# A macaron block's first layer: a new order of its slots, split sums for two of the FFN's products, and a norm moved to ScalarE

## The chip, the cores and the metric

The kernel runs on one core of a Trainium2 chip. The metric is the device time of one execution in microseconds. The core has TensorE (PE), VectorE (DVE), ScalarE (ACT), GpSimd (POOL) and SyncE (SP), which here only issues DMAs. Each engine runs its own list of instructions in order, and they meet through semaphores. All inputs and outputs are f32. About 0.2% (2 us) is what a measurement of this kernel can tell from no change.

## The reference, cut to what matters

```python
x = x + 0.5 * ffn0(layernorm(x))          # shared FFN with 8 LoRA experts, top 2
x = x + attn0(layernorm(x))               # gated linear attention, MLP behind it
x = x + 0.5 * ffn0(layernorm(x))
x = x + 0.5 * moe(layernorm(x))           # 8 experts, top 1
x = x + attn1(layernorm(x))
x = x + 0.5 * moe(layernorm(x))

def ffn0(x):                              # D=128, F=512, E=8, R=16, K=2
    t = rmsnorm(x) * norm_w
    probs = softmax(t @ gate_w.T)         # the best two, renormalised
    h1 = t @ w1.T + 2 * (t @ a1[e].T) @ b1[e].T
    h3 = t @ w3.T + 2 * (t @ a3[e].T) @ b3[e].T
    act = silu(h1) * h3
    out_e = act @ w2.T + 2 * (act @ a2[e].T) @ b2[e].T
    return sum over the two experts of weight_e * out_e
```

attn0 has the gates i, f = sigmoid(h @ Wi + bi), sigmoid(h @ Wf + bf) and o = sigmoid(h @ Wo + bo); its scores are a recurrence along the sequence. There are 4096 tokens of 128 values: eight sequences of 512. The output is x.

## The kernel before, in words

Tokens are worked on in chunks of 512, one sequence each, and x stays in SBUF. The first layer is the first three lines of the reference. Its two ffn0 passes over 8 chunks make 16 FFN items; the attention of a chunk lies between its two FFN items. All of it is one software pipeline: `SLOTS` holds slots m = -2 to 18, and `Slot` (line 56) says which item of which stage a slot works on: statistics (`stat`, item m+2), routing to the experts (`pre`, m+1), the products (`main`, m), the end of the item before (`tail`, m-1), six stages of attention (m-1 to m-6), and three of the second layer's routing (m-9 to m-11). So slots 6 to 9 hold everything of the attention, slots from 9 on also the routing, and slots 16 to 18 only ends.

The order within a slot is written out by hand, once for each engine: PE from line 623, ACT from line 999, DVE from line 1365, POOL from line 1711. A step there is a call such as `h(1, 3)`; each begins with its semaphore waits, so an engine that waits in one step holds up all steps behind it. SP loads x and all weights at the start, then zeroes the DRAM rows into which the routing scatters (line 309), then feeds the expert tiles.

For an FFN item, `h(1, k)` and `h(3, k)` (line 383) make h1 and h3 for step k of eight: four 128-row blocks j of F times two choices e. The choices are not computed per expert: u = a1 @ t for all 8 x 16 adapter rows is multiplied with a mask of the chosen expert (`ua` for the first choice) and by the difference of the two masks (`ud`), so that the second choice only adds its difference on top of the first in PSUM. These products are made in f32r with operands split into a high and a low part: `mm3` (line 361) is high*high + high*low + low*high. ACT makes silu, DVE `act(k)` (line 1190) multiplies with h3 and then with the choice's weight `wT`.

The two weighted activations of a block j, `act_[0][j]` and `act_[1][j]`, are then used in three ways, all in plain f32: POOL adds them to `gsum` (`total`, line 1639) and PE multiplies it with w2 (`down(j)`, line 425, bank BOUT); PE multiplies the first with a2 (`value(0, ...)`, first values, at the end of the slot) and the second with a2 (`value(1, ...)`, second values, in the next slot). DVE masks the values of either choice into `r1` and `r2`, POOL adds them, PE multiplies with b2 (`lora_out`), the result is transposed back and DVE adds half of it to x.

```python
def mm3(dst, w, m, start, stop, **more):
    mm(dst, w[0], m[0], start=start, stop=False, **more)
    mm(dst, w[0], m[1], start=False, stop=False, **more)
    return mm(dst, w[1], m[0], start=False, stop=stop, **more)
```

For the item one ahead, DVE normalises the rows (`f_norm`, line 1205, first in its slot), PE transposes them (`pre_T`), ACT saves them as f32 and as the high part, POOL makes the low part (`low`). PE makes `logits`, DVE picks the two experts (`top2`), ACT makes their weights from a tanh (`slot_weights`), PE transposes the choices into masks (`mask`), ACT saves them, POOL makes their difference (`mask_diff`), PE makes u (`up`), DVE masks it (`masked`), ACT and POOL split it (`up_high`, `up_low`).

For attention, `a_gate(0..3)` (line 593) makes the three gates and the values on PE, all through bank BSIDE each after ACT has saved the one before (`a_gates`, line 964, sigmoid); `a_scans` on DVE runs the recurrences; `a_den`, `a_back`, `a_mix` divide and add; `a_mid_T`, `a_mid`, `a_out`, `a_out_back` are the MLP. Routing has `r_norm`, `r_T`, `r_aff`, `r_top1`, `r_rank`, `r_rows`, `r_scatter`. PSUM has eight banks: two for h1, two for h3, BV (4) for values and the routing's transposes, BSIDE (5) for attention and routing, BOUT (6), BPRE (7) for the item ahead.

After the slots come small products of the second layer's weights (`products`), 23 expert tiles, the second attention and 23 tiles again.

## Time and profile before

| what | us |
|---|---|
| median of 3 runs | 1050.17 (1050.05 to 1051.02) |
| the profiled execution's own time | 1054.69 |
| its span, first to last instruction | 1053.0 |
| PE busy in it | 980.6 (93%) |
| DVE busy | 711.2 (68%) |
| ACT busy | 507.9 (48%) |
| POOL busy | 500.1 (47%) |
| mean granted TensorE clock | 0.992 of full speed |

Busy is the time in which an engine had an instruction under way. Matmuls are pipelined: a matmul's span is longer than the distance to the next one's start, so what PE takes for one is read from starts. In the trace an f32 matmul stands as two instructions, an f32r one as one. A number in brackets after an instruction is the engine's idle time before it with what ended it.

### The profile page before, as it was taken

How to read it: one execution, taken by the hardware profiler on the slowest of the kernel's cores; microseconds unless marked ns; L12 is line 12 of the kernel's file. 1: busy time of each engine (PE TensorE's matmuls, PEld its weight loads, DVE VectorE, ACT ScalarE, POOL GpSimd, SP SyncE). 2: the span in 40 equal slices, each digit the busy share in tenths (PEclk: the TensorE clock that was granted, in tenths of full speed). 3: DMA queues.
4: the chain of work that ended last, by engine and by line, in shares of the span. 5: the costliest groups of instructions: out<-in, count | busy, mean ns of one | idle time of the engine just before them, and what ended most of it. 6: DMA issues, size and time to landing. Idle time of an engine off the chain costs nothing. (4 is left out here: it accounts for less than half of the span.)

```text
span 1053.0 us, 15574 instructions
## 1 busy us (share of the span) xinstructions
PE 980.6 (93%) x4429; PEld 669.9 (64%) x4429; DVE 711.2 (68%) x2140; ACT 507.9 (48%) x1039; POOL 500.1 (47%) x485
## 2 busy tenths in 40 slices
PE   3999999999999999999999999899988999889993
PEld 2766667656565665656566656477864667648873
DVE  5787779788786877879797776445543667634542
ACT  3433454655646556564453332144534777515451
POOL 3456555554535545354654655524451155423443
PEclk9999999999999999999999999999999999989997
DMA  6069000000000000000000002146534000015651
GB/s 181 1 284 415 3 1 1 1 1 1 1 0 2 0 1 1 1 0 1 12 3 9 11 11 71 39 137 197 166 94 140 1 22 22 22 42 178 194 174 34
DMA packets 42900, 65.12 MB, mean 62 GB/s; under 512 B 7153, under 2 KB 25121, under 8 KB 40640
## 3 DMA queue, kind: packets, MB, share of 16 engines
q1 hardware_dynamic: 37824, 55.59, 16.1%
q0 software_dynamic: 4992, 8.54, 2.4%
q8 instruction: 36, 0.59, 0.2%
q14 instruction: 48, 0.39, 0.1%
HBM read 37.20 MB, written 28.74 MB: 63 GB/s over the span
## 5 line engine op out<-in xcount | busy, mean ns | idle before, releaser
L362 PE MATMUL bank<-split 128*128 128x512 f32 x416 | 206.9, 497 | 7.8 <-DVE ud L1267 4.1
L364 PE MATMUL bank<-split 128*128 128x512 f32 x416 | 165.2, 397 | 0.0
L363 PE MATMUL bank<-split 128*128 128x512 f32 x416 | 164.8, 396 | 0.0
L863 ACT ACTIVATE sil<-bank 128x512 f32<-128x512 f32 x128 | 76.2, 595 | 116.0 <-PE bank L364 115.2
L1644 POOL TENSOR_TENSOR gsum<-act 128x512 f32<-128x512 f32 x64 | 84.9, 1327 | 81.5 <-DVE act L1203 81.4
L421 PE MATMUL bank<-act,a 128*128 128x512 f32 x256 | 117.6, 592 | 0.0
L362 PEld LDWEIGHTS bank<-split 128*128 128x128 f32 x416 | 79.5, 191 | 48.8 <-issue 17.4
L1199 DVE TENSOR_TENSOR act<-bank,sil 128x512 f32<-128x512 f32 x128 | 87.8, 686 | 17.2 <-PE bank L364 14.2
L363 PEld LDWEIGHTS bank<-split 128*128 128x128 f32 x416 | 79.9, 192 | 28.3 <-issue 18.6
L688 PE MATMUL bank<-xlT,e 128*128 128x256 f32 x368 | 91.2, 392 | 5.1 <-ACT xlT L1068 2.7
L1203 DVE TENSOR_TENSOR act<-act,wT 128x512 f32<-128x512 f32 x128 | 91.7, 716 | 4.4
L364 PEld LDWEIGHTS bank<-split 128*128 128x128 f32 x416 | 79.2, 190 | 18.1
L704 PE MATMUL bank<-hT_e,e 128*128 128x256 f32 x368 | 87.3, 380 | 1.1 <-DVE oT_e L1534 1.1
L1068 ACT ACTIVATE xlT<-bank,lnb,lng 128x256 f32<-128x256 f32 x46 | 25.9, 564 | 119.0 <-PE bank L696 119.0
L1747 POOL DMA_INDIRECT rows_in<-yw,slot_i x64 | 62.9, 983 | 34.7 <-issue 18.8
L688 PEld LDWEIGHTS bank<-xlT,e 128*128 128x128 f32 x368 | 67.9, 194 | 16.5 <-issue 4.5
L1754 POOL DMA_INDIRECT out<-ob,ids x46 | 45.2, 983 | 66.9 <-DVE ob L1542 57.1
L1754 POOL DMA_INDIRECT rows_out<-ob,ids x46 | 45.2, 983 | 63.4 <-DVE ob L1542 55.6
L421 PEld LDWEIGHTS bank<-act,a 128*128 128x128 f32 x256 | 47.5, 190 | 42.0 <-issue 33.7
L704 PEld LDWEIGHTS bank<-hT_e,e 128*128 128x128 f32 x368 | 66.7, 191 | 8.7 <-issue 1.5
L431 PE MATMUL bank<-gsum,w 128*128 128x512 f32 x128 | 65.2, 600 | 0.5 <-POOL gsum L1644 0.5
L1529 DVE TENSOR_SCALAR hT_e<-bank,eb1T 128x256 f32<-128x256 f32 x92 | 40.3, 479 | 27.6 <-PE bank L688 27.2
(283 smaller groups left out, 1957.6 us busy)
## 6 DMA issues: line engine op xcount, KB each, us to landing
e<-e_dram SPq DMA_DIRECT2D x92, 256.0 KB, 3.1
rows_in<-yw SPq DMA_DIRECT2D x17, 1056.0 KB, 17.8
xin<-rows_in SPq DMA_DIRECT2D x46, 132.0 KB, 3.0
x<-rows_out SPq DMA_DIRECT2D x8, 256.0 KB, 4.7
rows_in<-yw,slot_i POOLq DMA_INDIRECT x64, 2.3
rows_out<-ob,ids POOLq DMA_INDIRECT x46, 2.3
out<-ob,ids POOLq DMA_INDIRECT x46, 2.4
act<-b_dram SPq DMA_DIRECT2D x2, 256.0 KB, 3.1
```

Of the source, the lines that this page charges most:

```text
L362: mm(dst, w[0], m[0], start=start, stop=False, **more)
L363: mm(dst, w[0], m[1], start=False, stop=False, **more)
L364: return mm(dst, w[1], m[0], start=False, stop=stop, **more)
L421: last = mm(bank[BV][:, :], a2[:, j, :], act_[e][j][:, :], start=j == 0, stop=j == J - 1)
L431: mm(bank[BOUT][:, :], w2[:, j, :], gsum[j % 2][:, :], start=j == 0, stop=False).then_inc(w2_used.sem, 1)
L688: last = mm(bank[2 * p + j // 2][:, (j % 2) * Q:(j % 2 + 1) * Q], w[:, rows(j)], xlT[p][:, :], start=True, stop=True)
L704: last = mm(bank[4][:, 0:Q], w[:, j, :], hT_e[p][:, j, :], start=j == 0, stop=j == J - 1)
L863: af(sil[(k - 1) % 2][:, :], bank[BH1[STEPS[k - 1][0] % 2]][:, :], ACT.Silu).then_inc(silu_done.sem, 1)
L1199: v.tensor_tensor(a[:, :], bank[BH3[j % 2]][:, :], sil[(k - 1) % 2][:, :], ALU.mult).then_inc(act_done.sem, 1)
L1203: v.tensor_tensor(a[:, :], a[:, :], wT[g % 2][e][:, :], ALU.mult).then_inc(weighted.sem, 1)
L1644: pool.tensor_tensor(out=gsum[j % 2][:, :], in0=act_[0][j][:, :], in1=act_[1][j][:, :], op=ALU.add).then_inc(summed.sem, 1)
L1754: pool.indirect_dma_start((rows_out, o)[n3 // NT], bass.IndirectOffsetOnAxis(ids[n3 % 4][:, q:q + 1], 0), ob[n3 % 4][:, q, :], None, bound ...
```

## The change

It does the following; the rest of the kernel, from the expert tiles on, is as before.

- The sum of the two weighted activations is written over the second (`act1[j]`), and ACT and POOL split it into a high and a low part (`sums_high`, `sums_low`). `down` and the second values use it with split w2 and a2 in three f32r passes. The second values are made of the sum: with masks m0 and m1, r = m1 * (a2 @ sum) - (m1 - m0) * (a2 @ first). First values are masked with the difference `mdT`.
- `down` for blocks 2 and 3 moves to the next slot, ahead of the second values.
- w2 and a2 are split in slot 0 (`sum_weights`, `sum_weights_low`).
- `f_norm` moves from DVE to ACT, at the end of the slot before, as x * scale + bias, with a product on POOL for the bias.
- The gates are sigmoid(z) = 0.5 * tanh(z/2) + 0.5: a tanh from PSUM (`gates_saved`), then a copy in place with scale and bias (`gates_done`). They are spread over the slot's second half.
- The MLP of the attention goes through BV, the routing's transposes through BSIDE.
- The order of each engine's slot is new. On POOL the row scatter moves to the next slot.
- `constants_for_routing` runs before the first slot instead of behind slot 1; the rows' zeroing follows slot -1 instead of slot 0. The weights of the second attention and the expert biases are loaded after the last slot's h (`late_loads`), into room that the split weights held.

```diff
+        LOW_DVE, LOW_POOL, LOW_LATE = (0, 1, 3, 5), (2, 4), (6, 7)
...
+                def value_sum():
+                    if l is None:
+                        return
+                    pe.wait_ge(*r_done(l, 1))
+                    pe.wait_ge(*sum_low(l))
+                    if l == 0:
+                        pe.wait_ge(weight_rest.sem, len(LOW_POOL) + 2)
+                    for j in range(J):
+                        last = mm3(bank[BV][:, :], tuple(w[:, rows(j)] for w in a2s), gs[j], j == 0, j == J - 1)
+                    last.then_inc(v_ready.sem, 1)
...
-                    pe.wait_ge(*summed(g, j + 1))
-                    mm(bank[BOUT][:, :], w2[:, j, :], gsum[j % 2][:, :], start=j == 0, stop=False).then_inc(w2_used.sem, 1)
+                    pe.wait_ge(*sum_low(n, j + 1))
+                    mm3(bank[BOUT][:, :], tuple(w[:, rows(j)] for w in w2s), gs[j], j == 0, False)
```

PE's order (its `fill` steps, which do something only from slot 16 on, left out):

```diff
-                h(1, 1); h(3, 1)
+                h(1, 1)
+                pre_T()
+                h(3, 1)
                 a_T()
                 h(1, 2)
+                logits()
+                if q == 0:
+                    up(0); up(1)
+                down(l, 2)
+                h(3, 2)
                 a_den()
-                h(3, 2)
-                pre_T()
+                down(l, 3)
+                value_sum()
                 a_back()
-                value(1, range(J))
                 h(1, 3)
                 r_aff()
                 h(3, 3)
-                logits()
                 a_out()
                 h(1, 4); h(3, 4)
                 lora_out()
                 a_out_back()
-                h(1, 5); h(3, 5)
+                h(1, 5)
+                mask(0)
+                h(3, 5)
                 back()
                 a_mid_T()
                 r_T()
+                mask(1)
                 h(1, 6)
                 a_mid(0)
+                mask(2)
                 h(3, 6)
-                mask(0)
-                down(0)
+                down(g, 0)
+                a_gate(0)
+                h(1, 7)
+                if q != 0:
+                    up(0)
                 a_mid(1)
-                h(1, 7)
-                mask(1)
                 h(3, 7)
+                down(g, 1)
+                a_gate(1)
                 a_mid(2)
-                down(1)
-                mask(2)
                 r_rank()
                 h(1, 8)
                 if q != 0:
-                    up(0)
+                    up(1)
+                a_gate(2)
                 h(3, 8)
-                value(0, (0, 1))
-                a_gate(0)
-                if q != 0:
-                    up(1)
-                value(0, (2, 3))
-                a_gate(1)
-                down(2)
-                a_gate(2)
-                down(3)
+                value((0, 1))
                 a_gate(3)
+                value((2, 3))
```

New or changed on ACT (guards for slots without the item left out):

```diff
+                def sums_high(n, j):
+                    act.wait_ge(*summed(n, j + 1))
+                    act.wait_ge(*v_ready(n - 1))
+                    af(gs[j][0], act1[j][:, :], ACT.Copy).then_inc(sum_high.sem, 1)
...
+                def f_norm():
+                    act.wait_ge(*rstd_f(n))
+                    act.wait_ge(*ynT_f(n - 1))
+                    for t in range(T):
+                        last = af(yn_f[:, t, :], xc(n)[:, t, :], ACT.Identity, bias=nb_f[n % 2][:, t:t + 1], scale=sc_f[n % 2][:, 1, t:t + 1])
...
+                    af(dst[:, :], bank[BSIDE][:, :], ACT.Tanh, bias=half[:, i:i + 1], scale=0.5).then_inc(gates_saved.sem, 1)
+                    act.wait_ge(*gates_saved(n, i + 1))
+                    af(dst[:, :], dst[:, :], ACT.Copy, scale=0.5, bias=0.5).then_inc(gates_done.sem, 1)
```

The new orders, whole, several steps to a line. ACT:

```
silu(1); pre_T(); sums_high(l, 3); a_T(); silu(2); sum_weights(); a_mid_norm(); silu(3); a_norm(0)
r_norm(s.r_pre) if s.m <= MAINS; slot_weights(); a_out(); silu(4); out_T(); silu(5)
sums_high(g, 0); mask(0); a_mid_T(); r_alpha(s.r_sort); r_T(s.r_pre, BSIDE); mask(1); silu(6)
sums_high(g, 1); a_mid(0); mask(2); mask(3); a_gate(0); silu(7); a_mid(1); a_gate(1); a_mid(2)
silu(8); up_high(0); a_gate(2); up_high(1); f_norm(); a_norm(1); sums_high(g, 2)
a_square(0); a_square(1); a_square(2); r_norm(s.r_stat) if s.m >= MAINS
```

DVE:

```
r_factors(s.r_pre); act(1); split_low(LOW_DVE[:2]); top2(0); act(2); a_den(); top2(1)
split_low(LOW_DVE[2:]); second_values(); a_mix(); r_read(s.r_sort, BSIDE); a_mid_stats(); act(3)
r_top1(s.r_sort); act(4); a_add(); f_stats(); act(5); f_add(); a_stats(); act(6)
r_stats(s.r_stat, xf_done, NCH); a_leaky(0); masked(0); act(7); masked(1); act(8)
a_leaky(1); r_rows(s.r_sort, BSIDE); a_leaky(2); a_scans(); first_values()
```

POOL:

```
sums_low(l, 3); low(); r_scatter(lane(s.m - 12, NCH)) if s.m <= MAINS; values(); a_sum()
a_mid_scale(); total(0); total(1); sum_weights_low(); sums_low(g, 0); f_scale(); mask_diff()
sums_low(g, 1); a_scale(); r_scale(s.r_stat); up_low(0); total(2); up_low(1); total(3)
sums_low(g, 2); a_product(); r_scatter(s.r_sort) if s.m >= MAINS
```

Before, a slot's DVE order began with `f_norm()` and had `r_rows` and `masked(0)` between act(7) and act(8), `masked(1)` behind act(8); POOL's had `total(2); total(3); up_low(0); up_low(1)`, with each `total` also waiting for the w2 product two blocks back.

## Rows read from the trace of the kernel before

**Rows 1.** The page: busy time by engine, and granted clock in 40 slices.

```profile
PE 980.6 (93%) x4429; PEld 669.9 (64%) x4429; DVE 711.2 (68%) x2140; ACT 507.9 (48%) x1039; POOL 500.1 (47%) x485
...
PEclk9999999999999999999999999999999999989997
```

**Rows 2.** Windows: stretch, length, busy PE, PEld, DVE, ACT, POOL, clock, DMA.

```profile
286.60:331.50 44.90, 44.50 (x178) 27.95 (x177) 35.11 (x87) 26.58 (x49) 22.55 (x19) 1.00 0.00 1
...
467.00:509.00 42.00, 40.32 (x178) 26.57 (x177) 39.97 (x106) 20.47 (x40) 19.33 (x18) 1.00 0.00 2
```

**Rows 3.** Timeline of PE in a full slot: start, time, instruction, count.

```profile
329.36 0.39 PE L362 MATMUL bank<-split 128*128 128x512 f32 x1
...
331.42 0.60 PE L358 MATMUL bank<-ident,yn_a 128*128 128x128 f32 x4
...
336.69 3.60 PE L421 MATMUL bank<-act,a 128*128 128x512 f32 x8
...
340.36 0.40 PE L363 MATMUL bank<-split 128*128 128x512 f32 x1
```

**Rows 4.** Groups by line: count, busy us, mean ns, idle before; and line 886.

```profile
L863 ACT ACT_TABLE_LOAD x9 | 11.5, 1283 | 0.2
...
L971 ACT ACT_TABLE_LOAD x8 | 10.3, 1283 | 0.8 <-PE bank L609 0.7
...
L886 ACT ACTIVATE th<-dlt 128x4 f32<-128x4 f32 x16 | 3.2, 200 | 19.1 <-DVE dlt L1257 19.1
...
L1644 POOL TENSOR_TENSOR gsum<-act 128x512 f32<-128x512 f32 x64 | 84.9, 1327 | 81.5 <-DVE act L1203 81.4
...
L1203 DVE TENSOR_TENSOR act<-act,wT 128x512 f32<-128x512 f32 x128 | 91.7, 716 | 4.4
L1199 DVE TENSOR_TENSOR act<-bank,sil 128x512 f32<-128x512 f32 x128 | 87.8, 686 | 17.2 <-PE bank L364 14.2 <-issue 1.9 <-ACT sil L863 0.7
L1212 DVE TENSOR_SCALAR yn_f<-x,mv_f,sc_f 128x128 f32<-128x128 f32 x64 | 48.9, 852 | 1.3 <-POOL sc_f L1657 1.2
```

**Rows 5.** Timeline of PE at the end of a full slot: value half, gates.

```profile
321.54 1.88 PE L421 MATMUL bank<-act,a 128*128 128x512 f32 x4
...
328.90 0.39 PE L363 MATMUL bank<-split 128*128 128x512 f32 x1
```

**Rows 6.** PE's waits from 80 to 660 us; timeline of DVE at 500 us.

```profile
PE bank L362 <- DVE ud L1267: 4.1, 3, 1.6
...
500.53 1.11 DVE L1461 TENSOR_TENSOR pos<-pos,oh 128x32 f32<-128x32 f32 x1
```

**Rows 7.** Timeline of ACT at the end of a full slot.

```profile
327.48 0.62 ACT L914 ACTIVATE split<-ua 128x512 fp32r<-128x512 f32 x1
...
328.52 1.64 ACT L983 ACTIVATE yn_a<-x,nb_a,sc_a 128x128 f32<-128x128 f32 x4
330.18 1.28 ACT L863 ACT_TABLE_LOAD   x1
331.47 0.60 ACT L863 ACTIVATE sil<-bank 128x512 f32<-128x512 f32 x1
```

**Rows 8.** Timeline: the first norm; the routing constants, first and last of 21.

```profile
5.68 1.04 POOL L1657 TENSOR_TENSOR sc_f<-sc_f,neghalf 128x4 f32<-128x4 f32 x1 [3.52 <-DVE sc_f L1175]
...
6.76 1.11 DVE L1212 TENSOR_SCALAR yn_f<-x,mv_f,sc_f 128x128 f32<-128x128 f32 x4 [1.24 <-POOL sc_f L1657]
...
91.19 0.34 POOL L1771 MEMSET region<- 128x1 f32 x8
...
93.67 0.18 POOL L1788 CAST place<-place_i 128x2 f32<-128x2 int32 x1
```

**Rows 9.** Timeline at the last FFN item: matrix load, second values, POOL's addition.

```profile
646.91 0.43 SPq L320 DMA_DIRECT2D e<-e_dram  x1
...
652.29 3.60 PE L421 MATMUL bank<-act,a 128*128 128x512 f32 x8
...
656.70 1.26 POOL L1650 TENSOR_TENSOR r<-r 128x512 f32<-128x512 f32 x1 [0.45 <-DVE r L1289]
```

More of the change, by code:

```diff
@@ L109, in build @@
         mv_f = [sb(f"mv_f{i}", [P, T]) for i in range(2)]; sc_f = [sb(f"sc_f{i}", [P, 2, T]) for i in range(2)]
+        nb_f = [sb(f"nb_f{i}", [P, T]) for i in range(2)]
         yn_f = sb("yn_f", [P, T, P])
@@ L411, in value, with down @@
+                def down(n, j):
                     if n is None:
                         return
[L413 to L421 removed]
@@ L897, in mask @@
                     if n == 0:
+                        act.wait_ge(*u_masked(q - 1))
+                    if n == 1:
                         act.wait_ge(*r_done(q - 2))
@@ L994, in a_T @@
                             af(w[:, :], wif[:, k:k + 1].to_broadcast([P, P]), ACT.Copy).then_inc(spread.sem, 1)
+                        af(half[:, 0:2], bif[:, :], ACT.Copy, scale=0.5).then_inc(spread.sem, 1)
+                        af(half[:, 2:3], vecs[:, 5:6], ACT.Copy, scale=0.5).then_inc(spread.sem, 1)
+                        act.wait_ge(spread.sem, 4)
                     act.wait_ge(*ynT_a(n))
@@ L1355, in a_scans @@
                         return
[L1356 removed]
+                    dve.wait_ge(*gates_done(n))
                     dve.wait_ge(*gates_ready(n))
```

321 lines of the change are left out of this document (176 added, 145 removed).

## The prediction

> **What bounds the kernel now.** I read the page first. TensorE is busy for 93% of the span and its clock is granted in nearly every slice until the expert tiles; no other engine is over 68% [rows 1]. The first layer, some 630 us of it, is one loop of slots, so I cut out slots with the table of windows. A full slot with attention (44.9 us) has PE busy for 44.5 us, DVE for 35.1, ACT for 26.6 and POOL for 22.6; the slot where routing overlaps the last attention chunks has PE at 40.3 of 42 and DVE at 40.0 [rows 2]. So PE's own work is what a slot is made of. Three things can change the time: how long PE's products take, what still makes PE wait inside a slot, and whether the new order makes another engine late.
>
> What a product takes is read from the distance of its starts, since the ends are modelled. Nine f32r passes lie between 329.36 and 331.42 us, so one takes 0.229 us. The eight instructions of the four plain f32 products start at 336.69; the f32r pass behind them is over when the next one starts, at 340.36. That is (340.36 - 336.69 - 0.229)/8 = 0.430 us each [rows 3]. A plain f32 product of 512 columns is two of these, 0.860 us; a product in three f32r passes is 0.687 us.
>
> **The products (a gain of 22.1 us).** Each of 16 chunks has four down products and four second values that go from f32 to three passes. The first values, the adapter's output and all of attention stay f32. 16 x 8 x (0.860 - 0.687) = 22.1 us, all on PE, the engine that sets the slot. Splitting costs ACT four copies and POOL four subtractions a chunk. A subtraction costs what the sum does, 1.3 us, so POOL goes from 22.6 to about 27.8 us a full slot, and ACT gains 4 x 0.52 of work [rows 2, 4, 7]. What hides them is slack: sum 3 is split at the end of a slot and sum 4 at the start of the next, and their down products are moved behind the logits, so that PE has some 6 to 9 us of other work while they are made. If that cover went, PE would wait through one copy and one subtraction, 1.8 us, per slot.
>
> **The gates (a gain of 8.9 us).** Now the four gates stand at the slot's end, each waiting for ACT to save the one before, the first save behind an activation-table load. From 321.54 to 328.90 - 0.229 us PE ran seven f32 products, 7.13 us for 7 x 0.860 = 6.02: 1.11 us are lost, in each of 8 slots [rows 5]. After the change the gates lie 3 to 5 us apart with passes of h between. ACT needs about 0.7 us from a gate's product to its save, so no wait is left: 8 x 1.11 = 8.9. Sigmoid becomes tanh, and the trace shows that tanh and silu need no load between them (16 calls on line 886, and only lines 863 and 971 reload), so 16 of the 17 reloads go, 20.5 us of ACT; the 24 second copies, SBUF to SBUF, give back 24 x 0.52 = 12.5 us [rows 4, 7]. The Trainium skill ("ScalarE: Activation LUTs", section on what a table load costs) has a switch of sets at about 2.66 us, the load and a drain. In this trace silu starts 1.29 us after its load does [rows 7], so the drain isn't seen and I count 1.28; neither would alter the sum, since ACT isn't the bound.
>
> **The late masks (a gain of 4.1 us).** Between the two halves of the first values PE waits for the masked u, because DVE does them behind the routing's row numbers, one of which sat 1.1 us. Three such waits make 4.1 us [rows 6]. In the new order u's first half is made after the seventh step and masked ahead of it, and the row numbers go behind. The waits should vanish; at worst they stay.
>
> **The FFN's norm on ACT (no gain of its own).** DVE loses 64 instructions, 48.9 us, 3.1 us a slot; at 0.85 us each they were slow beside the first ones (4 in 1.11 us). ACT gets four of the kind that it does in 1.64 us, and POOL one small product of 0.2 us [rows 4, 7, 8]. This takes DVE off the 40 of 42 us above, without a step of PE's that hangs on it.
>
> **The cost: ACT at the slot's seam (a loss of 3.2 us).** PE now wants the transposed rows almost at once: logits stand behind h(1,1), the transposes, h(3,1), hT and h(1,2), which is 3 x 6 x 0.229 + 2 x 0.45 = 5.0 us into the slot. ACT must have saved the rows, and ahead of that in its queue stand silu 8, two pairs of splits, the gate, the two norms, a sum's split, three squares and silu 1. By the steps between ACT's starts (0.52 for an SBUF copy, 0.6 for silu, 1.64 for a norm [rows 7]) this is 0.6 + 1.04 + 1.25 + 1.04 + 1.64 + 1.64 + 0.52 + 1.56 + 0.6 + 1.3 = 11.2 us. It starts with silu 8, about 6.1 us before the seam, and so ends at 5.1. With the latency of two semaphores PE waits some 0.25 us; and the attention's output product then waits about 0.15 us for DVE's mix, which follows the second values. 0.4 x 8 slots = 3.2 us. Behind the waiting logits stand down product 3, h(3,2) and all that follows, and DVE's first choice of experts stands in front of act(2). The bounds: none, if ACT runs ahead, and 2 us a slot, 16 in all, if ACT's waits for DVE inside this queue add up.
>
> **The start (a loss of 0.8 us), the end and the rest (nothing).** The routing constants now stand before the first slot. They took 91.19 to 93.85 us, 2.7 us, and POOL is idle for 3.5 us there [rows 8]: hidden, by 0.8 us. If it weren't, every us over counts in full. ACT's norm takes 1.64 for DVE's 1.11 and waits for one POOL product more: 0.5 + 0.3 = 0.8 us. The table load ahead of it just moves forward. Seven late weight loads stand before the expert matrices on SP, at 0.43 us an issue [rows 9]: 3 us, hidden because the first tile can only be read when slot 18 has scattered its rows; without that cover they would count 3 us. At the end, slot 16 takes the last sums: POOL, ACT, POOL, then one down product and the four value products, where now the values take 652.29 to 655.72. This adds about 1 us; act(8) no longer waits behind the row numbers, 2 us earlier, but four scatters of 1.27 us now stand before POOL's addition, which now starts at 656.70 right behind such scatters [rows 9]. I put the sum at nothing, between -1.5 and +3.
>
> **Sum.** -22.1 - 8.9 - 4.1 + 3.2 + 0.8 = -31.1 us. The profiled execution took 1054.7 us, 1.7 more than its span, and 4.5 more than the median of the runs; taken from the median, 1050.2 - 31.1 = 1019 us.
>
> **Rivals.** (a) **DVE and POOL in each other's way.** DVE's product of two SBUF tiles (line 1203) has a mean of 716 ns, the one with a PSUM input 686 ns, and small DVE operations of 0.16 us take 1.1 when POOL is at work; POOL gets 64 more long ones [rows 4, 6]. The Trainium skill ("SBUF — State Buffer", section on who interferes with whom) has DVE products of two SBUF inputs contend with GpSimd's reads, an argument against this change. If the delays grow so that act(k) comes late, PE waits 1 us or so a slot: 16 us back, 1035 us. For it: DVE is dense in the slots with routing. Against: DVE sheds 3.1 us a slot that were themselves the slowest of this kind. 0.14. (b) **The splitting comes late.** A down product waits for its chain DVE, POOL, ACT, POOL; at 1.3 us a slot the products' gain is gone, and 1050 - 31 + 21 = 1040 us is left. POOL's queue is long at the seam (both lows of u, sum 3, sum 4, two splits, the attention's product). 0.09. (c) **Slower: ACT is late at the seam.** The same place as my cost, but in every slot and larger: if f_norm, behind the second pair of splits, waits for DVE's masks and silu 1 is pushed with it, PE stands at logits. The gain without this cost is 34 us, so from 34/16 = 2.1 us a slot the change is no gain; at 3 us it costs 48 and the time is 1064 us. ACT's total (26.6 + 4 x 0.52 + 3 x 0.52 + 1.64 - 2 x 1.28 = 29.3 us of 43) speaks against it; the order alone could do it. 0.04. (d) **The change does less than it says**: PE's transition from f32 to f32r costs as much as a pass saves. The starts show no such loss now. 0.02, at 1041 us.
>
> **Numbers.** The forecast has 0.71. The range: downward, the seam at no cost, a better end, and small waits of 0.3 us a slot gone give 1010; upward it takes in (a) and half of (b), with 10 us of the seam's bound: 1037. What is within 0.2% (2 us) of now, about what a measurement of this kernel can tell from no change, is reached only between (b) and (c): 0.02. Faster 0.94, slower 0.04.
>
> **What would show it.** Right: PE's busy time some 20 us less, a full slot at 42 to 43.3 us instead of 44.9, no idle time before the gates' line, two activation-table loads left of 18 in the first layer, DVE under 36 us in the 42 us slot. Wrong: idle time of PE released by ACT's split (the rows' save) before logits, or by POOL's sum splits before the down and value products; DVE over 90% of a slot; or the first transposes later than 9.5 us.

## The result, and the profile after

The change makes the kernel slower: 1062.18 us (median of 5 runs, 1056.79 to 1062.88) against 1050.17 (1048.82 to 1051.53) for the kernel before on the same chip; the ratio is 1.0104, 95% interval [1.0077, 1.0132]. The forecast was 1019.

The profiled execution of after was the fastest of its five, 1056.79 us with a span of 1055.1; that of before took 1054.69 with 1053.0. So the two traces differ by 2.1 us of the 12 us between the medians. They show the mechanism; the size comes from the medians.

The page of after, busy time by engine and the granted clock, to be held against [rows 1]:

```profile
PE 957.4 (91%) x4557; PEld 699.1 (66%) x4557; DVE 737.4 (70%) x2076; ACT 551.0 (52%) x1179; POOL 608.6 (58%) x567
PEclk8999999999999999999898999999999999999998
```

TensorE (PE) is busy for 23 us less, about as forecast, in a span that isn't shorter. POOL has 108 us more. In the 20th and the 22nd slice (501 to 528 and 554 to 580 us) the clock isn't full, where before it was.

I then cut the first layer of both kernels by windows, from the first silu to the last. The columns are stretch, length, busy time (count) of PE, PEld, DVE, ACT, POOL, clock, DMA share and GB/s. Before:

```profile
28.00:57.50 29.50, 29.50 (x120) 20.72 (x120) 23.55 (x49) 10.82 (x21) 14.71 (x13) 1.00 0.00 1
57.50:160.00 102.50, 102.48 (x416) 68.01 (x415) 80.71 (x187) 45.16 (x84) 56.24 (x65) 1.00 0.44 180
160.00:465.00 305.00, 300.88 (x1197) 189.11 (x1196) 240.56 (x603) 178.01 (x319) 154.61 (x125) 1.00 0.00 1
465.00:645.80 180.80, 175.63 (x761) 118.95 (x760) 150.03 (x382) 76.24 (x147) 94.13 (x81) 1.00 0.02 7
645.80:1053.00 407.20, 361.09 (x1905) 265.21 (x1904) 200.40 (x875) 185.93 (x451) 168.91 (x179) 0.98 0.33 99
```

And after:

```profile
30.60:63.00 32.40, 28.24 (x126) 20.88 (x126) 25.53 (x45) 16.54 (x33) 21.52 (x18) 0.99 0.92 378
63.00:160.00 97.00, 94.62 (x427) 70.91 (x426) 81.35 (x176) 52.76 (x109) 69.37 (x57) 1.00 0.16 64
160.00:462.30 302.30, 289.43 (x1262) 203.10 (x1262) 261.80 (x575) 191.33 (x380) 204.41 (x162) 1.00 0.00 1
462.30:650.50 188.20, 177.05 (x797) 131.94 (x796) 153.17 (x367) 88.32 (x179) 125.92 (x103) 0.95 0.02 7
650.50:1055.00 404.50, 356.22 (x1912) 264.01 (x1910) 202.75 (x876) 187.22 (x453) 171.95 (x181) 0.99 0.33 101
```

This is the account of the two traces. From first to last silu, before takes 617.8 us with PE busy for 608.5, so PE stands for 9.3. After takes 619.9 with 589.3 busy, and stands for 30.6: **21.3 us of new standing**. Its busy time fell by 19.2, and it would have fallen by more, since the last of these stretches ran at a clock of 0.95: the trace has it at half for 3.4 us from 468, for 6.8 us from 512 and from 557, and for the first 0.5 us from 30.6, together 17.5 us in which 8.8 us of full-speed work is lost. Before had its own half clock, though its first window says 1.00: the clock's record in that trace starts only at 31.8 us, and until 31.6 us its passes start 0.43 us apart, then 0.23. That loses 1.8 us. So PE's work fell by 19.2 + 8.8 - 1.8 = 26.2 us, and 21.3 + 8.8 - 1.8 = 28.3 us eat it. The first silu comes 2.6 us later (30.6 for 28.0), and what follows the last is 2.7 us shorter (404.5 for 407.2), although only because before has half clock for 6.8 us at 940, which loses 3.4 us, and after none behind its last silu. That is -26.2 + 28.3 + 2.6 - 2.7 = +2.0, the spans' difference of 2.1.

By slots, counted from one first silu to the next, the four full ones (6 to 9) take 44.9 to 45.1 us in before and 43.9 to 44.2 in after, where 42 to 43.3 were forecast. Slots 11 and 12 take 42.0 and 40.1 in before, 48.5 and 44.6 in after: 10.9 us more in these two alone.

What PE waited for from 20 to 660 us (who waits, on whom, us in total, times, longest). Of before, [rows 6] has the largest, 4.1 us; its whole list makes 13.9 us. The six largest of after, of 38.4 in all:

```profile
PE bank L374 <- POOL split L1700: 10.7, 9, 2.3
PE bank L370 <- DVE iv L1413: 6.6, 5, 1.6
PE bank L481 <- ACT split L898: 6.1, 2, 3.0
PE bank L374 <- POOL split L1738: 4.0, 1, 4.0
PE bank L495 <- ACT mT L939: 3.1, 4, 1.6
PE bank L374 <- DVE ud L1319: 2.5, 4, 0.8
```

Line 1700 is POOL's split of the sums. 2.5 us of its waits lie in slot 0, the others behind the starts of slots 1, 4, 5, 11, 15 and 16; none is in a full slot. Line 481 is the logits, on ACT's save of t. These two are the "wrong" signs that the prediction named.

Line 370's wait, which it didn't see, is 1.3 to 1.6 us in each full slot and in slot 10. There attention's transposes write the bank from which DVE still reads the values: line 1413 makes `iv`, the values times the input gate, between its two scans. Ahead of it stand the leaky steps (the MLP's activation, `a_leaky`) and the first scan:

```profile
368.09 3.45 DVE L1394 SCALAR_TENSOR_TENSOR msq<-msq 128x512 f32<-128x512 f32 x2
371.47 2.32 DVE L1412 TENSOR_TENSOR_SCAN den<-gf,gi 128x512 f32<-128x512 f32 x1
373.71 0.72 DVE L1413 SCALAR_TENSOR_TENSOR iv<-bank,vecs,gi 128x512 f32<-128x512 f32 x1
374.57 0.63 PE L370 MATMUL bank<-ident,yn_a 128*128 128x128 f32 x4 [1.27 <-DVE iv L1413]
```

Why DVE and POOL are late is in the groups of lines. DVE's weighting, its product out of PSUM and its leaky step (before: 716, 686 and 684 ns, [rows 4] for the first two):

```profile
L1266 DVE TENSOR_TENSOR act<-act,wT 128x512 f32<-128x512 f32 x128 | 119.2, 931 | 4.4
L1394 DVE SCALAR_TENSOR_TENSOR msq<-msq 128x512 f32<-128x512 f32 x24 | 33.4, 1410 | 0.0
L1412 DVE TENSOR_TENSOR_SCAN den<-gf,gi 128x512 f32<-128x512 f32 x8 | 18.2, 2280 | 0.1
L1262 DVE TENSOR_TENSOR act<-bank,sil 128x512 f32<-128x512 f32 x128 | 87.8, 686 | 55.0 <-PE bank L376 28.7 <-issue 24.2 <-ACT sil L887 1.9
```

Those with an operand in PSUM kept their time. The three that read two operands in SBUF and touch no PSUM got longer; the scan had 1623 ns in before. Not everything of DVE between SBUF tiles did: the statistics of x (`BATCH_NORM_STATS2`, one input) stayed at 278 ns. The timeline of the seam between slots 11 and 12 (where one slot's end meets the next one's start) shows how the three get longer, and what it led to:

```profile
507.09 1.29 POOL L1738 TENSOR_TENSOR split<-ud,split 128x512 fp32r<-128x512 f32 x1
508.33 1.30 POOL L1694 TENSOR_TENSOR act<-act 128x512 f32<-128x512 f32 x1
508.39 1.80 DVE L1394 SCALAR_TENSOR_TENSOR msq<-msq 128x512 f32<-128x512 f32 x1
509.11 0.39 PE L376 MATMUL bank<-split 128*128 128x512 f32 x1
509.59 1.72 POOL L1700 TENSOR_TENSOR split<-act,split 128x512 fp32r<-128x512 f32 x1
510.11 0.68 DVE L1334 TENSOR_TENSOR r<-bank,mdT 128x512 f32<-128x512 f32 x1
510.22 0.63 ACT L1012 ACTIVATE msq<-msq 128x512 f32<-128x512 f32 x1 [3.08 <-DVE msq L1394]
510.75 0.58 ACT L887 ACTIVATE sil<-bank 128x512 f32<-128x512 f32 x1
511.80 0.69 ACT L898 ACTIVATE split<-bank,normw 128x512 fp32r<-128x512 f32 x1
...
512.54 1.88 PE L481 MATMUL bank<-gate,tT 128*128 128x8 f32 x8 [3.05 <-ACT split L898]
514.27 0.77 PE L374 MATMUL bank<-split 128*128 128x512 f32 x1
514.84 0.63 PE L375 MATMUL bank<-split 128*128 128x512 f32 x1
515.27 0.63 PE L376 MATMUL bank<-split 128*128 128x512 f32 x1
```

DVE's leaky step starts at 508.39, just after POOL's sum. POOL is done at 509.6, DVE 0.6 us later; POOL's next operation, from 509.59, takes 1.72 for its usual 1.3. The two take turns. PE's last pass of the slot starts at 509.11. ACT stands for 3.08 us on that step, with silu 1 and t queued behind it, and PE stands for 3.05 us at the logits. Then the passes lie 0.43 us apart in place of 0.23: half clock, which this trace grants for 6.8 us from 512.4.

### The profile page after: what moved, and what is told of

Its sections match the earlier page's. It is cut to its first block and busy times, and to the rows that moved or that the text cites. A ratio compares the mean times of both kernels' runs of the same rounds, so it can differ in the third digit from the quotient of the medians.

```text
span 1055.1 us, 16018 instructions
## 1 busy us (share of the span) xinstructions
PE 957.4 (91%) x4557; PEld 699.1 (66%) x4557; DVE 737.4 (70%) x2076; ACT 551.0 (52%) x1179; POOL 608.6 (58%) x567
## 5 line engine op out<-in xcount | busy, mean ns | idle before, releaser
L374 PE MATMUL bank<-split 128*128 128x512 f32 x544 | 254.3, 467 | 18.5 <-POOL split L1700 10.7
L376 PE MATMUL bank<-split 128*128 128x512 f32 x544 | 216.7, 398 | 0.0
L375 PE MATMUL bank<-split 128*128 128x512 f32 x544 | 216.1, 397 | 0.0
L374 PEld LDWEIGHTS bank<-split 128*128 128x128 f32 x544 | 104.4, 192 | 56.1 <-issue 16.2
L375 PEld LDWEIGHTS bank<-split 128*128 128x128 f32 x544 | 104.9, 193 | 30.0 <-issue 14.9
L1266 DVE TENSOR_TENSOR act<-act,wT 128x512 f32<-128x512 f32 x128 | 119.2, 931 | 4.4
L376 PEld LDWEIGHTS bank<-split 128*128 128x128 f32 x544 | 104.2, 192 | 24.0
L1694 POOL TENSOR_TENSOR act<-act 128x512 f32<-128x512 f32 x64 | 93.4, 1460 | 36.3 <-DVE act L1266 36.2
L1700 POOL TENSOR_TENSOR split<-act,split 128x512 fp32r<-128x512 f32 x64 | 93.8, 1468 | 13.8 <-ACT split L956 13.5
L712 PE MATMUL bank<-xlT,e 128*128 128x256 f32 x368 | 88.3, 383 | 5.4 <-ACT xlT L1131 2.7
L1738 POOL TENSOR_TENSOR split<-ua,split 128x512 fp32r<-128x512 f32 x32 | 47.9, 1496 | 46.6 <-ACT split L964 46.5
L430 PE MATMUL bank<-act,a 128*128 128x512 f32 x128 | 58.8, 592 | 0.0
```

The source lines that it names most:

```text
L712: last = mm(bank[2 * p + j // 2][:, (j % 2) * Q:(j % 2 + 1) * Q], w[:, rows(j)], xlT[p][:, :], start=True, stop=True)
L1266: v.tensor_tensor(a[:, :], a[:, :], wT[g % 2][e][:, :], ALU.mult).then_inc(weighted.sem, 1)
L1694: pool.tensor_tensor(out=act1[j][:, :], in0=act0[j][:, :], in1=act1[j][:, :], op=ALU.add).then_inc(summed.sem, 1)
L1700: pool.tensor_tensor(out=gs[j][1], in0=act1[j][:, :], in1=gs[j][0].bitcast(F32), op=ALU.subtract).then_inc(sum_low.sem, 1)
```

## The experiments

All ratios are to the kernel before, run on the same chip.

**The squares out of ACT's queue at the seam.** They go from the slot's end (after) into the next slot, behind t:

```
-                a_square(0); a_square(1); a_square(2)    # behind sums_high(g, 2)
...
                 pre_T()
+                a_square(0); a_square(1); a_square(2)    # of the chunk in its next slot
                 sums_high(l, 3)
```

> The changed kernel with ACT's three squares moved out of the slot's end, to behind the save of the transposed rows in the next slot. Theory A (ACT's queue at the slot's seam holds up the logits, and the wait lets TensorE's clock fall): in the changed kernel's profile PE waited 6.1 us in two slots before logits for ACT's split, behind squares that waited for DVE; the clock was at half for 6.8 us behind each. Both waits should shrink to under 1 us, the granted clock stay at 1.0 from 500 to 570 us, and the time fall from 1062 by 8 to 14 us, to 1048 to 1054. Theory B (POOL's longer queue and its collisions with DVE are the whole cost): the waits only move to the next step that hangs on DVE or POOL, and the time changes by less than 3 us, 1059 to 1063.

Measured: 1054.2 us median (1048.45 to 1056.09), ratio 1.0042 [1.0022, 1.0062]. The logits' wait is gone, and slots 11 and 12 go from 48.5 and 44.6 us to 46.2 and 41.0. The clock still falls three times, but for 3.4 us each, two of them in the stretch where theory A had none. By the ratios the move gives back 6.5 of the 11 us lost, less than the 8 to 14 expected. The rest isn't in this wait.

**The gates alone, in the kernel before:** sigmoid as tanh with a second copy, the order untouched.

```
-                        af(dst[:, :], bank[BSIDE][:, :], ACT.Sigmoid, bias=bias)
+                        af(dst[:, :], bank[BSIDE][:, :], ACT.Tanh, bias=half[:, i:i + 1], scale=0.5)
+                        act.wait_ge(*gates_saved(n, i + 1))
+                        af(dst[:, :], dst[:, :], ACT.Copy, scale=0.5, bias=0.5)
```

> The kernel before with one part of the change alone: the gates as a tanh and a copy, in their old places. The forecast's term for the gates was 8.9 us in all. The table load stood before the first gate's save in each of 8 slots; the first gate's wait made some 4.9 us of the 8.9, the fixed steps of the other gates the rest. If the gates' term was right, this part gives 3 to 6 us, 1044 to 1047, with no sigmoid table loads in the trace. Rival: ACT isn't what PE waits for there, and the added copies and the loads cancel: 1049 to 1051.

Measured: 1047.66 us (1044.26 to 1049.53), ratio 0.998 [0.9964, 0.9996]. By the ratio a gain of 2.1 us, 0.4 to 3.8 by its interval: less than the 3 to 6 expected of this part. The gates' places, the other part of the forecast's 8.9, are untouched here. The waits say why it is small; the gates' own wait (3.6) is gone, and PE stands one step later, at the transposes behind the scans:

```profile
PE bank L362 <- POOL split L1677: 3.8, 1, 3.8
PE bank L358 <- DVE iv L1366: 3.2, 7, 0.5
PE bank L362 <- DVE ud L1272: 3.1, 2, 1.6
```

Full slots stay at 44.9 us. So the gates, the scans and the transposes of the next chunk are a chain with little slack, even before the change.

**The new order without the sums' splits:** down and second values as plain f32 products, ACT's and POOL's splits of the sums left out.

```
-                    pe.wait_ge(*sum_low(n, j + 1))
-                    mm3(bank[BOUT][:, :], tuple(w[:, rows(j)] for w in w2s), gs[j], j == 0, False)
+                    pe.wait_ge(*summed(n, j + 1))
+                    mm(bank[BOUT][:, :], w2[:, rows(j)], act1[j][:, :], start=j == 0, stop=False)
```

> The changed kernel with its new order, but the sum isn't split: the down products and the second values are plain f32 again, 128 products of 0.860 us in place of 0.687; ACT's 64 copies and POOL's 64 subtractions are gone. If the three passes gave what the forecast said (22.1 us) and the splitting cost little, this is slower than the changed kernel: 1075 to 1085. Theory B (POOL's 64 more operations cost as much as the passes save, through late splits and through DVE operations stretched from 0.7 to 1.5 us): about the same or faster, 1050 to 1063, with the mean of DVE's weighting back from 0.93 to about 0.75 us.

Measured: 1056.66 us (1053.52 to 1061.48), ratio 1.0063 [1.0039, 1.0087]. It is not slower than the change (1.0104), as the first theory had it, and lies in theory B's 1050 to 1063.

In PE's work the three passes give what was forecast. Full slots take 45.27 us, 1.3 to 1.4 more than with the splits (43.9), where eight products at 0.173 make 1.38; both have the same wait of 1.3 us on `iv`. **But as time almost nothing of it is left over the first layer:** from first to last silu the profiled executions take 622.6 us without the splits and 619.9 with them, 2.7 us for a forecast of 22.1, because PE's waits from 20 to 660 us make 21.1 us without and 38.4 with them. The two other large waits stand here as well, so it is the new order that makes them, not the splits:

```profile
PE bank L367 <- DVE iv L1402: 6.4, 5, 1.3
PE bank L476 <- ACT split L893: 6.0, 2, 3.0
```

The waits for the masked u, 4.1 us in before, are gone here, and 2.5 us of them come back with the splits. In slots 0 and 1 the splits lose: 26.3 and 31.9 us without, 29.9 and 32.4 with them.

45.27 is also 0.3 to 0.4 more than in before (44.9), with the gates' change in it: the new order alone costs. The gates themselves gain in it. PE is busy for 43.90 us of a full slot in place of 44.45, and its 0.4 us ahead of the gates are gone, together 0.95 of the 1.11 forecast; the 1.3 us at the transposes take more than that.

DVE's leaky step still takes 1407 ns here, with POOL busy for 519.9 us in place of 608.6. So the new orders stretch it, not the sums' splits: two of its three steps stand behind act(8), where POOL now makes the sums and the splits of u without a gap. The weighting has 841 ns, between before's 716 and after's 931; theory B had 750.

**The sums' low halves on DVE in place of POOL:**

```
-                    pool.tensor_tensor(out=gs[j][1], in0=act1[j][:, :], in1=gs[j][0].bitcast(F32), op=ALU.subtract)
+                    v.tensor_tensor(gs[j][1], act1[j][:, :], gs[j][0].bitcast(F32), ALU.subtract)
```

> The changed kernel with the low parts of the sum made by DVE (64 operations of some 0.7 us) and not by POOL (64 of 1.47 us). Theory B: POOL's queue shortens by 5.9 us a slot, the waits for its splits (10.7 us) go, and DVE's operations meet it less: 1045 to 1056. Theory A: the seam is bound by DVE and ACT, DVE gets 2.8 us more a slot, and it is no better or worse: 1060 to 1070.

Measured: 1062.35 us (1060.88 to 1062.77), ratio 1.0124 [1.0093, 1.0154]; no better than the change, as theory A had it. The splits take 977 ns on DVE, its leaky step still 1406, and PE now waits for DVE's splits, oftener:

```profile
PE bank L374 <- DVE split L1333: 12.3, 15, 2.4
PE bank L481 <- ACT split L898: 6.0, 2, 3.0
```

**The row numbers behind the leaky steps** (after, VectorE's order alone):

```
                 a_leaky(1)
-                r_rows(s.r_sort, BSIDE)
                 a_leaky(2)
+                r_rows(s.r_sort, BSIDE)
```

> The changed kernel with VectorE's row numbers of routing put behind the leaky step of the second and third middle tile; nothing else. Theory (VectorE late at the seam of slots 11 and 12 makes ScalarE's squares, and with them t and the logits, late, and the clock falls after that wait): the logits' wait of 6.1 us (two of 3 us) goes, and with it most of the half clock at 512 and 557 us; 1057 to 1062 us fall to 1049 to 1053, slots 11 and 12 from 48.5 and 44.6 to 46.3 and 42 us, about what the squares' move gave. Rival (the row numbers don't matter, the leaky steps are slow by themselves): the logits still wait 2 us or more twice, and the time stays within 2 us of the changed kernel's. Both: the wait for the scans (6.6 us) stays.

Measured: 1055.26 us (1051.83 to 1056.96), ratio 1.0043 [1.0025, 1.0061]. The wait for t falls from 6.1 to 1.0 us (two of 0.5), and the ratio is that of the squares' move. The two edits cut the same chain in two places: row numbers, leaky step, square, silu 1, t. The median is 2 us over the expectation's upper end.

**Both, and attention's transposes behind the logits:**

```
                 h(3, 1)
-                a_T()
                 h(1, 2)
                 logits()
                 down(l, 2)
+                a_T()
```

> The changed kernel with three moves: ScalarE's squares behind t in the next slot, VectorE's row numbers behind the leaky steps, and the transposes of the normalised first layer (TensorE and ScalarE) behind the logits. Theory (the waits at the seam are what the change lost): no wait for the scans' first product, none for t at the logits, no half clock in slots 8 to 14; full slots 42.5 to 43.3 us in place of 43.9; the time about 1040 us (1037 to 1045), under the kernel before. Rival (VectorE is full there, as SBUF operations stand behind GpSimd's): the waits only move to the next reader (up's masks, the affinities), and the time is that of the squares' move alone, 1052 to 1056.

Measured: 1058.04 us (1052.25 to 1063.47), ratio 1.0061 [1.0036, 1.0086]: a miss, the rival's way, and beyond its price. The first two waits went as expected. But the transposes, and their wait, had stood ahead of the third down product while its split was made. Now PE reaches the down product first and waits for POOL, 14 times for 19.5 us. The second line is a stretch of 46 us from 325 to 371, most of it in the longest full slot:

```profile
PE bank L374 <- POOL split L1700: 19.5, 14, 2.0
```

```profile
325.00:371.00 46.00, 43.95 (x173) 30.98 (x172) 34.93 (x79) 26.00 (x53) 28.53 (x22) 0.89 0.00 1
```

A wait of 2.0 us, and a clock of 0.89 in a slot that had it full. Full slots take 45.7 us, 1.8 more than in after, one of them 49.1, and the clock falls in each of the five slots from 201 to 431 us: for 3.4 us in four of them, which costs 1.7, most of the difference. In four of the five the wait ahead of it was only 1.5 or 1.6 us.

**The leaky steps out of the seam.** Steps 1 and 2 go into the next slot, behind DVE's first activation, and the squares behind silu 2:

```
+                act(1); a_leaky(1); a_leaky(2)          # DVE, at the slot's start
...
-                a_leaky(1)
                 r_rows(s.r_sort, BSIDE)
-                a_leaky(2)
                 a_scans()
```

> The changed kernel with the leaky step of the second and third middle tile taken out of the seam into the next slot, behind its first activation, and the squares behind ScalarE's second silu there. Theory (an operation of VectorE whose operands are all in SBUF waits for the end of GpSimd's running one; the seam has GpSimd busy without a break, so each such operation put there costs 1.7 us, not 0.7): the scans start 3.4 us earlier, the wait of 6.6 us for their first product and that of 6.1 us for t at the logits go, no half clock in slots 8 to 14; 1037 to 1045 us. The leaky steps take 0.7 to 1.7 us in the new place, as GpSimd works there too. Rival: they delay the second activation and the splits of VectorE, TensorE then waits for the third product by 1 us or more in each full slot, and the time is 1050 or more.

Measured: 1054.56 us (1049.41 to 1059.38), ratio 1.0044 [1.0025, 1.0063]. The scans' wait and the logits' wait are gone and full slots take 43.5 us, but line 1700 has 11.3 us. The leaky step still takes 1315 ns: POOL is busy at the slot's start as well. The time is the rival's (1050 or more). The wait that it named is there too, 0.7 to 1.1 us in each full slot, where after had none; but it is POOL that is late. At 369.51 to 378.51 us it runs sum, two splits of u, sum and the sum's split without a gap, and PE starts the down product when that split is done. In after the 1.3 us at the transposes had stood in front of this wait and hidden it.

**Three small moves at the start, on top of that:** ACT's table loaded by a silu of four numbers ahead of the first slot, POOL's split of w2 and a2 ahead of the first sum, down product 3 behind h(3, 2).

```
             act.wait_ge(*constants(0))
+            af(th[:, :], neghalf[:, 0:T], ACT.Silu)
...
+                sum_weights_low()
                 total(0)
...
+                h(3, 2)
                 down(l, 2)
-                h(3, 2)
```

> As the kernel with the leaky steps in the next slot, and three small moves at the start: ScalarE's function table loaded during the first loads (a silu of four numbers before the first slot), GpSimd's split of w2 and a2 ahead of the first sum, and the third down product behind the third h product. Theory (these three are on the path in the first slots, 1.3 to 2.6 us, 2.5 us and 1 to 2.5 us in turn): 5 to 7 us under the kernel without them, first silu at 28.0 us in place of 30.6. Rival (the first slots are bound by routing's masks anyway): only the table's 1.3 to 2.6 us show.

Measured: 1047.59 us (1043.89 to 1054.02), ratio 0.9987 [0.9966, 1.0008]: 7.0 us under the kernel without them, at the upper end of what was expected. The first silu comes at 27.8 us in place of 30.6, so the table load alone is 2.8; the first two slots give another 1.2. In the traces another 3.9 us come from slot 5 (44.2 to 40.4 us), where the kernel without them had 6.8 us of half clock; which slots the clock strikes isn't explained by these moves.

**The clock held.** After, with ten idle bf16 products of 512 columns ahead of the logits in slots 12 and 13:

```
                 h(1, 2)
+                if s.m in (12, 13):
+                    pe.wait_ge(*act_done(g, 0))
+                    hold(10, BH3[1])
                 logits()
```

> The changed kernel, with ten products of 512 columns in bf16, whose result nobody reads, put ahead of the logits in slots 12 and 13, where TensorE waits 3 us for t each time. Theory (a wait of 2 to 3 us costs twice: once itself, and once more through the clock, at half for 6.8 us behind it): the waits still end at the same times, the granted clock stays full there, slots 12 and 13 become 2 to 3.4 us shorter each, and the time falls by 5 to 7 us against the changed kernel's (1057 to 1062), to 1050 to 1056. Rival (the clock falls for the whole stretch's load, or at chance): the clock falls there or in the neighbour all the same and the time stays within 2 us; or the fillings come late and add up to 4 us.

Measured: 1055.18 us (1053.62 to 1058.66), ratio 1.0048 [1.0029, 1.0066], as the theory had it. By windows, first after, then this kernel, over slots 11, 12 and 13:

```profile
462.00:511.00 49.00, 44.60 (x202) 32.27 (x200) 43.99 (x103) 23.91 (x49) 32.34 (x26) 0.97 0.00 1
511.00:555.00 44.00, 41.58 (x177) 30.40 (x177) 33.24 (x81) 22.62 (x47) 27.23 (x24) 0.92 0.02 7
555.00:593.00 38.00, 35.44 (x153) 26.34 (x154) 28.82 (x77) 18.03 (x37) 23.95 (x21) 0.91 0.02 8
```

```profile
462.00:511.00 49.00, 44.79 (x204) 32.23 (x203) 42.30 (x102) 23.36 (x47) 30.97 (x25) 0.97 0.00 1
511.00:555.00 44.00, 43.20 (x201) 30.08 (x200) 36.40 (x84) 24.14 (x49) 30.37 (x25) 1.00 0.02 7
555.00:593.00 38.00, 36.77 (x178) 27.29 (x176) 31.84 (x83) 20.14 (x41) 26.84 (x24) 1.00 0.03 8
```

The clock is full where it was 0.92 and 0.91, and the two slots shorten by 3.2 and 3.0 us (44.63 to 41.46 and 37.64 to 34.60); slot 11, ahead of them, is 1.7 longer. The waits still end when t is saved, so the half clock behind a wait of 3 us cost as much again. Work that does nothing made the kernel faster, by 5.9 us as the ratios have it (1.0104 and 1.0048), by 2.5 us in the traces, where this one has 3.4 us of half clock at 654 that after has not.

**Fillings on the best kernel so far:** six products ahead of the first mask, fourteen ahead of the first h product, eight in slot 16.

```
+                if g == 0:
+                    hold(14, BH3[1])
                 h(1, 1)
```

> The kernel with the leaky steps in the next slot and the three small moves at the start, and three fillings of TensorE with products nobody reads: six of 512 columns ahead of the first mask, fourteen ahead of the first h product, eight ahead of the third down product of slot 16. Theory: the half clock of 10.2 us at the start and of 3.4 us at 644 us go, 3 to 7 us less than without (1042.9 us span there, 1047.6 us median), so 1041 to 1045. Rival: the clock falls elsewhere instead, the time stays at 1046 to 1049.

Measured: 1050.59 us (1045.17 to 1059.2), ratio 1.0 [0.9972, 1.0027], where it was 0.9987 without the fillings: the rival, and 1.6 us beyond its range. The 10.2 us at half at the start became 3.4 and those at 644 are gone, but the profiled execution has the clock fall at 287, 331, 475 and 519 us, in slots that the edit doesn't touch; without the fillings it fell at 330 and 474 alone of these. The runs spread over 14 us, and here their mean granted clock goes with them: 1045.17 us at 0.988, 1059.2 at 0.979. A clock lower by 0.009 over 1050 us is 9.5 us, so most of this kernel's spread is clock.

**The affinities and the middle product later,** on top:

```
                 h(1, 3)
+                h(3, 3)
                 r_aff()
-                h(3, 3)
+                h(1, 4)
                 a_out()
-                h(1, 4); h(3, 4)
+                h(3, 4)
```

> As the kernel with the fillings, and the affinities put behind the third pair of h products and the middle product behind the fourth h product of the gate half (TensorE waited 2.3 us for z ahead of the affinities in slot 10, and 2 us for the row numbers' logits ahead of the middle product in slot 11). Theory (independent h products can stand in those waits): slots 10 and 11 go from 46.3 to 44 or 45, 2 to 4 us less. Rival: VectorE's top choice then comes later and the wait moves to the row ranks or to the back transposes; no change or 1 us more.

Measured: 1047.52 us (1042.75 to 1050.89), ratio 0.9965 [0.9947, 0.9982], 3.1 us under the kernel with the fillings. Slots 10 and 11 go from 46.3 and 47.9 to 45.6 and 45.6, in slot 11 with 3.4 us of half clock in place of 6.8; the 44 or 45 expected aren't reached. This is the fastest version of all these edits, 0.35% under the kernel before; the gates' change alone gave 0.2%, and the two intervals overlap.

**One spare POOL operation in the kernel before,** behind the third sum, on a tile that nobody reads:

```
                 total(2)
+                pool.tensor_tensor(out=spare[:, :], in0=spare[:, :], in1=spare[:, :], op=ALU.mult)
```

> The kernel before with one more GpSimd product of 128x512 elements in SBUF in each slot, behind the third sum, where GpSimd stood idle for 1.1 us; nobody reads it. Theory (an operation of VectorE whose operands are all in SBUF waits for the end of the GpSimd operation that runs, one with an operand in PSUM doesn't): VectorE's weighting and leaky step beside it go from 0.69 us to 1.2 to 1.8 us, its multiplications out of PSUM stay at 0.68 us, and the time rises by 0 to 1 us a full slot, 0 to 10 us in all. Rival (VectorE's longer times come from the data or the place): they stay at 0.69 us, and only the masked splits on GpSimd come 1.3 us later.

Measured: 1061.14 us (1054.89 to 1062.58), ratio 1.0085 [1.006, 1.011]. The timeline at 367 us, DVE and POOL:

```profile
366.75 0.68 DVE L1200 TENSOR_TENSOR act<-bank,sil 128x512 f32<-128x512 f32 x1
367.08 1.04 POOL L1725 TENSOR_TENSOR spare<-spare 128x512 f32<-128x512 f32 x1
367.47 1.20 DVE L1204 TENSOR_TENSOR act<-act,wT 128x512 f32<-128x512 f32 x1
368.59 0.68 DVE L1343 SCALAR_TENSOR_TENSOR msq<-msq 128x512 f32<-128x512 f32 x1
```

The product out of PSUM starts before the spare operation and runs past its start at 0.68 us. The weighting starts in its middle and ends 0.55 us after it: 1.20 us for its 0.69. The leaky step, which starts when POOL is done, takes 0.68; so it isn't stretched here; the expectation had it stretched. Full slots take 45.34 us in place of 44.85, and the 0.5 us show at PE as a wait of 0.9 for the gates in place of 0.4, behind DVE, ACT's squares and its table load. One operation in POOL's idle time, whose result nobody reads, costs 0.5 us in a full slot, 4.7 us to the last silu (650.5 for 645.8). The ratio says 9 us. The profiled execution has 3.4 us of half clock more at 690 and 10.2 at 946 for before's 6.8; but other runs took as long at a mean clock of 0.994 (1060.46 us), so the rest isn't explained.

## Why the prediction was wrong

What failed is what the sum put at nothing or next to it: the splits' cover, the seam and the transposes.

**The products: right as PE's work, wrong as time.** A full slot with and without splits differs by 1.3 to 1.4 us for 1.38. Of the 22.1 us, 21.1 lie ahead of the last silu; with the gates' 8 x 0.55 that is 25.5 of the 26.2 us of work that left PE. But this work became time only where nothing else made PE wait, 2.7 us of it in the traces. By the ratios the kernel with the splits is even 4 us slower than the one without, though the two intervals overlap.

**The splits' cover: the step that failed most.** "What hides them is slack" and "some 6 to 9 us of other work" was a sum of PE's work, not POOL's queue in front of the split. POOL goes through a sum, two splits of u, a sum and the split without a break, at 1.3 us each when alone and 1.7 to 2.2 when DVE takes its turn. PE waited 10.7 us for the split itself, and 17.3 us more in all than without the splits. That is rival (b), at 0.09: half its price of 21 us by the first number, most of it by the second. Its mechanism was told as it came.

**The gates: gained, and lost one step later.** The step "no wait is left: 8 x 1.11 = 8.9" is right of the gates, for which PE doesn't wait in after. It took what left them for time won. Behind them comes the chain through the scans to the transposes, which the sum didn't follow.

**The transposes' bank: not seen.** They kept their place behind h(3, 1), and so had a condition that the sum never named: DVE's read of the same bank. In before the scans waited for the gates and came in time. Now the gates are early, but two leaky steps of 1.7 us stand ahead of the scans, and the first scan takes 2.3 us for 1.6: 6.6 us of waits.

**The late masks: half right.** The new order did away with the 4.1 us, as the kernel without split sums shows; with the splits 2.5 us are back.

**ACT at the seam: failed.** The sum of 11.2 us counted ACT's own operations and forecast 0.25 us at the logits. It left out that ACT's squares wait for DVE's leaky steps, which wait for POOL. The bound, "if ACT's waits for DVE inside this queue add up", stated it; I took the low end. The chance went to every slot at once (rival (c), 0.04). What happened is its mechanism in two slots, 11 and 12, the only ones where DVE has both the leaky steps and the row numbers at the seam: 6.1 us at the logits, and 6.8 more through the clock, 12.9 for the 3.2 forecast. That doubling stood nowhere in the prediction.

**DVE and POOL in each other's way: right in kind.** This was rival (a), 0.14. The rule of the Trainium skill that it named ("SBUF — State Buffer", section on who interferes with whom) agrees with the runs: beside the spare operation the weighting took 1.20 us for 0.69, the product out of PSUM 0.68. The rival looked for the delay in act(k); it came in the leaky step and the scan. The mean of before, 716 ns, hid it: it mixed operations beside an idle POOL with some beside a busy one. And the leaky step went from 684 to 1410 ns by the new orders alone, with the splits or without. Mean DVE busy time isn't what it costs; the cost is what queues behind.

**The start: mis-sized.** 0.8 us forecast, 2.6 measured to the first silu. The first norm and its table load cost what was forecast: t is saved from 11.36 us in place of 10.43. What the sum left out is the second item's norm, which now stands in ACT's queue at 27.68, 1.6 us long, ahead of the first silu and its table load. Loading the table early gave 2.8 us back.

**The end: within its bounds.** 2.7 us less behind the last silu; without before's half clock there it would be 0.7 more.

Put together as an estimate, -31.1 + 17.3 (the splits) + 9.7 (the seam) + 6.6 (the transposes) + 1.8 (the start) - 2.7 (the end) is +1.6 us, where the traces have +2.1.

What stays open is the rest, 10 of the 12 us between the medians. The profiled execution of after was its fastest, so they were not seen in a trace. The clock is an obvious candidate, but the five runs of after don't bear it out: the fastest, 1056.79 us, had a mean clock of 0.982, and 1062.18 us had 0.986. Open too is which stretches lose the clock. Of the three falls in the slots of after, two follow a 3 us wait; the one at 468 follows a wait of 1.6. The same wait of 1.6 at 330 is followed by none, and neither are two waits of 2.0 in the kernel with the small moves at the start (514 and 555 us).

## What to carry to other kernels

When work is taken off the engine that bounds a loop and put on others, add up the queue in front of each thing that it waits for, across engines, in order; shares of busy time don't show it. Look for stretches in which POOL has no gap, and put no VectorE operation there that takes two operands from SBUF and none from PSUM, above all none that a third engine waits for. A wait of TensorE may be paid twice, by the clock behind it: here both waits of 3 us at the logits were, in after and in two of its variants, and many of 1.5 to 2.3 us, but others of that length weren't. Cover it with real work. Idle products in the place of two 3 us waits won time; spread over other places they won none.

## What the runs showed that I had not expected

- A DVE product, weighting or leaky step of 128x512 between SBUF tiles that starts while a long POOL operation runs ends 0.55 us after POOL's: 1.2 to 1.8 us for 0.68. A small one ends with POOL's: the 128x32 product at 506.20 us took 0.98 us, to 507.18, and POOL's ended at 507.12. POOL's next one is longer by 0.4 us. With an operand in PSUM it is not touched (686 ns in both kernels).
- Half clock lasted 3.4, 6.8 or 10.2 us while PE had work, and 3.4 us of it cost 1.7. The kernel with the transposes' move, with the same work but more short waits, had it in nine slots, before in none from 32 to 940 us.
- The runs spread over 6.0 us in 29 runs of before and over 14 us in 12 runs of the kernel with the fillings. In that one the mean clock goes with the time; in 29 runs of before it hardly does.
